# Inverse head norms by one 64-column power on GpSimd and one bounding operation on VectorE, in place of a seed and three Newton steps; row selection one slot later

## The reference

```python
def _head_rmsnorm(x, gamma):
    norm = jnp.linalg.norm(x, axis=-1, keepdims=True)
    normed = x / jnp.maximum(norm, 1e-12)
    scale = (gamma + 1.0) * DIM_HEAD ** 0.5
    return normed * scale[None, :, None, :]
...
x = _rmsnorm(tokens, norm_w)
q = x @ Wq
kv = x @ Wkv
...
q = _head_rmsnorm(q, q_gamma)
k = _head_rmsnorm(k, k_gamma)
sim = jnp.einsum('bhid,bhjd->bhij', q, k)
sim = jnp.tanh(sim / SOFTCLAMP) * SOFTCLAMP * DIM_HEAD ** (-0.5)
out = jnp.einsum('bhij,bhjd->bhid', softmax(sim), v)
```

## Time and profile before

| | |
|---|---|
| median of 3 runs | 1172.26 us (1169.23 to 1201.33) |
| the profiled execution | 1171.93 us, its span 1170.0 us |
| granted TensorE clock, mean | 0.996 |
| PE busy | 1053.4 us (90%) |
| ACT busy | 1033.3 us (88%) |
| DVE busy | 932.8 us (80%) |
| POOL busy | 853.8 us (73%) |

### The profile page before, as it was taken

One profiled execution on the slowest core, in us unless ns is written; L12 is line 12 of the kernel. 1 busy time (PEld: TensorE's weight loads), 2 busy tenths in 40 slices (PEclk: granted clock), 3 DMA queues, 4 the chain that ended last, 5 costly groups with the idle time before them and its releaser, 6 DMA issues.

```text
span 1170.0 us, 33883 instructions
## 1 busy us (share of the span) xinstructions
PE 1053.4 (90%) x12873; PEld 833.1 (71%) x12873; DVE 932.8 (80%) x2185; ACT 1033.3 (88%) x1543; POOL 853.8 (73%) x784
## 2 busy tenths in 40 slices
PE   3779999999999999999999999999999999999987
PEld 2457777777777777777777777777777777777766
DVE  5887878887878878878878878878888878888862
ACT  2689999999999999999999999999999999999886
POOL 6577777778778777778777778777778777778654
PEclk9899999999999999999999999999999999999999
DMA  4244443334433333434334433334333334343341
GB/s 142 42 78 67 77 74 77 68 74 74 77 77 74 70 70 78 74 75 77 72 66 79 76 72 79 66 74 79 74 72 78 71 69 83 70 75 70 71 81 33
DMA packets 310743, 86.45 MB, mean 74 GB/s; under 512 B 282036, under 2 KB 309816, under 8 KB 310584
## 3 DMA queue, kind: packets, MB, share of 16 engines
q1 hardware_dynamic: 310584, 84.30, 37.7%
HBM read 12.13 MB, written 4.19 MB: 14 GB/s over the span
## 4 chain that ended last, share of the span: by engine, by line
ACT 34%; PE 26%; DVE 26%; issue 12%; DMA 0%; POOL 0%; ACTq 0%
ACT clamped L569 12%; PE ps_scores L492 9%; DVE qk L764 7%; ACT probs L576 7%; PE ps_aux L467 5%; DVE halves L728 5%; ACT oT L608 4%; ACT L613 4%; DVE o_sb L741 3%; PE ps_y L542 3%; DVE v_lo L769 3%; DVE norm L679 3%; ACT hid L613 3%; PE ps_y L540 3%; PE ps_aux L426 2%
## 5 line engine op out<-in xcount | busy, mean ns | idle before, releaser
L931 POOL TENSOR_TENSOR probs_lo<-probs 128x1024 f16<-128x1024 f32 x256 | 484.7, 1893 | 270.3 <-ACT probs L576 270.3
L569 ACT ACTIVATE clamped<-ps_scores 128x1024 f32<-128x1024 f32 x256 | 265.9, 1039 | 67.2 <-PE ps_scores L492 66.9
L576 ACT ACTIVATE probs<-clamped 128x1024 f32<-128x1024 f32 x256 | 275.4, 1076 | 1.0 <-PE ps_o L522 0.4
L728 DVE TENSOR_TENSOR halves<-ps_n,halves 128x512 f16<-128x512 f32 x256 | 175.1, 684 | 99.3 <-ACT halves L584 99.2
L520 PEld LDWEIGHTS ps_o<-v_hi,probs 128*128 128x128 bf16 x2048 | 184.7, 98 | 90.0 <-issue 87.5
L520 PE MATMUL ps_o<-v_hi,probs 128*128 128x65 bf16 x2048 | 214.0, 195 | 33.2 <-DVE ps_n L720 23.1
L492 PE MATMUL ps_scores<-heads_T 64*128 64x256 f16 x3072 | 212.8, 271 | 6.9 <-ACT clamped L569 4.7
L521 PE MATMUL ps_o<-v_lo,probs 128*128 128x64 bf16 x2048 | 212.2, 193 | 0.0
L522 PE MATMUL ps_o<-v_hi,probs_lo 128*128 128x65 bf16 x2048 | 211.9, 194 | 0.0
L426 PE MATMUL ps_aux<-w_hi,xhT_hi 128*128 128x512 f32 x384 | 174.4, 454 | 40.0 <-DVE v_lo L769 25.6
L521 PEld LDWEIGHTS ps_o<-v_lo,probs 128*128 128x128 bf16 x2048 | 187.5, 99 | 0.0
(11 more groups left out here) (80 smaller groups left out, 1919.4 us busy)
## 6 DMA issues: line engine op xcount, KB each, us to landing
heads_T<-halves SPq DMA_TRANSPOSE x512, 2.5
x_in<-in_L_attn_tokens_dram SPq DMA_DIRECT2D x32, 128.0 KB, 2.3
x_res<-in_L_attn_tokens_dram SPq DMA_DIRECT2D x32, 128.0 KB, 2.3
out_dram<-y_sb SPq DMA_DIRECT2D x32, 128.0 KB, 2.0
sel_raw<-xn SPq DMA_DIRECT2D x192, 4.0 KB
qk<-in_L_attn_Wkv_dram SPq DMA_DIRECT2D x2, 512.0 KB, 5.2
qk<-in_L_attn_Wq_dram SPq DMA_DIRECT2D x1, 512.0 KB, 4.0
qk<-in_L_ffn_W_dram SPq DMA_DIRECT2D x2, 256.0 KB
```

The costliest lines, as they stand in the source:

```text
L569: nc.scalar.activation(clamped[:].rearrange("p j n -> p (j n)"), ps_scores[:].rearrange("p j n -> p (j n)"), ACT.Tanh).then_inc(clamp_done, 1)
L576: nc.scalar.activation(probs[:, pair % RING].rearrange("p j n -> p (j n)"), clamped[:].rearrange("p j n -> p (j n)"), ACT.Exp, bias=LIFT, ...
L728: v.tensor_tensor(halves16[:, pair % 4, 1].rearrange("p a n -> p (a n)"), ps_n[:], halves16[:, pair % 4, 0].rearrange("p a n -> p (a n)"), ...
L931: g.tensor_tensor(probs_lo[:, buf].rearrange("p j n -> p (j n)"), probs[:, buf].rearrange("p j n -> p (j n)"), probs[:, buf].rearrange("p ...
```

## The change

The two seeds and the nine Newton operations are taken out of VectorE's list. GpSimd gets one instruction in slot 3, `norm_roots`: `norm2` to the power of -0.5, 128 x 64 elements, with the tile `minus_half` grown from 4 to 64 columns as its second input. VectorE gets one instruction in slot 4, `guard`: the minimum of the roots and 1e12, written to `rnorm`. `select` moves from slot 3 to slot 4 of GpSimd's list. The waits of PE on seeds and Newton operations go; the first `normalise` of a batch waits for the guard instead; the first sum of squares of a batch waits until the roots of the batch before are made.

```diff
 VECTOR_STEPS = [
...
-    [("halves",), ("sum", 6, 1), ("sum", 7, 1), ("divide",), ("normalise",), ("seed", 0), ("low", 1, 0), ("seed", 1)],
-    [("halves",), ("divide",), ("newton", 0), ("normalise",), ("newton", 1), ("newton", 2), ("newton", 3), ("newton", 4)],
-    [("halves",), ("divide",), ("newton", 5), ("newton", 6), ("newton", 7), ("newton", 8), ("normalise",), ("norm_stats",),
+    [("halves",), ("sum", 6, 1), ("sum", 7, 1), ("divide",), ("normalise",), ("low", 1, 0)],
+    [("halves",), ("divide",), ("normalise",)],
+    [("halves",), ("divide",), ("guard",), ("normalise",), ("norm_stats",),
      ("q", 0, 2)],
...
     [("bias",), ("lo",)],
+    [("roots",), ("lo",)],
     [("select",), ("lo",)],
-    [("lo",)],
     [("rstd",), ("lo",)],
...
-        minus_half = sb("minus_half", [P, 4])
+        minus_half = sb("minus_half", [P, TT * 2 * HEADS])
...
                 wait(pe, qk_normed, min(PAIRS * n + s - 1 + NORMALISE_LEAD + 1, PAIRS * batches))
-                if s == 3:
-                    wait(pe, seed_made, min(2 * (n + 2), 2 * batches))
-                if s in (4, 5):
-                    wait(pe, newton_step, min(9 * (n + 2) - (4 if s == 4 else 0), 9 * batches))
...
+                if k == 0:
+                    wait(dve, roots_made, b)
                 v.tensor_reduce(norm2[:, 8 * k:8 * k + 8], squares.rearrange("p (h d) -> p h d", d=DH),
                                 AX_X, ALU.add).then_inc(norm2_made, 1)
...
+            def guard(st):
 
                 b, _, _ = st.batch(1)
+                dve.wait_ge(roots_made, b + 1)
+                wait(dve, qk_normed, PAIRS * b)
+                v.tensor_scalar(rnorm, roots[:], NORM_MAX, None, ALU.min).then_inc(rnorm_made, 1)
 
             def normalise(st, ahead, pair):
...
                 if pair == 0:
-                    dve.wait_ge(newton_step, 9 * b + 9)
+                    dve.wait_ge(rnorm_made, b + 1)
...
+            def norm_roots(st):
+
+                b, _, _ = st.batch(1)
+                pool.wait_ge(norm2_made, 8 * b + 8)
+                wait(pool, rnorm_made, b)
+                g.tensor_tensor(roots[:], norm2[:], minus_half[:], ALU.pow).then_inc(roots_made, 1)
```

More of the change, by code:

```diff
@@ L41 @@
 RMS_EPS = 2.0 ** -23
-NORM2_MIN = 1e-24
-RSQRT_SEED = float(0x5F3759DF - (1 << 22) - (1 << 30))
+NORM_MAX = 1e12
 LIFT = 4.1588830833596715
@@ L208, in block_kernel @@
         norm2 = sb("norm2", [P, TT * 2 * HEADS])
-        newton_r = sb("newton_r", [P, TT * 2 * HEADS])
+        roots = sb("roots", [P, TT * 2 * HEADS])
         at = 4 * (DH + 1)
-        rnorm, minus_half_norm2, newton_a = [ps_o[:, at + i * TT * 2 * HEADS:at + (i + 1) * TT * 2 * HEADS] for i in range(3)]
+        rnorm = ps_o[:, at:at + TT * 2 * HEADS]
         halves16 = sb("halves16", [P, 4, 2, TT * 2, P], F16)
@@ L264, in block_kernel @@
         norm2_made = sem("norm2_made")
-        seed_made = sem("seed_made")
-        newton_step = sem("newton_step")
+        roots_made = sem("roots_made")
+        rnorm_made = sem("rnorm_made")
         q_scaled = sem("q_scaled")
@@ L678, in sum_squares @@
                     dve.wait_ge(k_squared, 4 * b + 2 * t + c - 1)
+                if k == 0:
+                    wait(dve, roots_made, b)
                 v.tensor_reduce(norm2[:, 8 * k:8 * k + 8], squares.rearrange("p (h d) -> p h d", d=DH),
                                 AX_X, ALU.add).then_inc(norm2_made, 1)
-            def seed(st, k):
+            def guard(st):
                 b, _, _ = st.batch(1)
[L685 to L709, removed]
+                dve.wait_ge(roots_made, b + 1)
+                wait(dve, qk_normed, PAIRS * b)
+                v.tensor_scalar(rnorm, roots[:], NORM_MAX, None, ALU.min).then_inc(rnorm_made, 1)
             def normalise(st, ahead, pair):
@@ L807, in run @@
                                 normalise(st, *now)
-                        elif what == "seed":
+                        elif what == "guard":
                             if "front" in st.stages:
[L810 to L813, removed]
+                                guard(st)
                         elif what == "norm_stats":
@@ L858, in norm_rstd @@
                 g.tensor_tensor(rstd[:].rearrange("p a b -> p (a b)"), var_eps[:].rearrange("p a b -> p (a b)"),
-                                minus_half[:], ALU.pow).then_inc(rstd_made, 1)
+                                minus_half[:, 0:2 * TT], ALU.pow).then_inc(rstd_made, 1)
             def norm_apply(st, ahead):
@@ L955, in run @@
                                 add_bias(st)
+                        elif what == "roots":
+                            if "front" in st.stages:
+                                norm_roots(st)
                         elif what == "select":
```

## The result

The changed kernel takes 1343.93 us in the median (1342.47 to 1345.01), 1.148 times the kernel before (95% interval 1.146 to 1.150): slower by about 173 us. Its profiled execution took 1343.59 us, with a span of 1341.8 us, 171.7 us more than that of the kernel before. One execution of the kernel before, of 1201.33 us, was a slow one and is left out of the ratio; the others took 1169.23 to 1172.26 us.

A forecast was written before the change was run, and what follows sets the result against it. PE (90% busy) and ACT (88%) were taken to share the bound. 1171.9 us now, plus 254 for 31 full steps of 8.2 us, plus 11 ahead of the first attention gave 1437 us; range 1165 to 1475.

The forecast's parts named there:

- cheap power: GpSimd slot 3: power up to 5 us, guard never waits, time as now, 1160 to 1190 us; chance 0.24.
- the case that I chose: GpSimd slot 3: power's cost goes by the column, 11 to 14.2 us, kernel at 1350 to 1475 us; chance 0.52.
- partly pipelined: GpSimd slot 3: power of 6 to 11 us, a step grows by it less about 5.9 us, 1190 to 1350; chance 0.18.
- What is taken from VectorE counts as nothing: VectorE slots 3 and 4: removing 2.3 us a step of Newton work gains nothing, at most 31.8 us over the run.
- faster: PE at slots 3 and 5: Newton operations held it up, both waits vanish, 1140 us; needs power under 5 us; chance 0.03.
- The length of the power: GpSimd slot 3, 64 columns: 13.7 us, from 0.19 us fixed plus 0.211 us a column; bounds 1.13 and 16.5.
- the upper end: GpSimd power: all of its cost is by the column with nothing fixed, 16.5 us for 64 columns.
- The walk of the step: One full step, GpSimd to PE: lo(3) 7.0 us late, values(4) 8.6 late, less 0.78 regained, so 7.8 us longer.
- The clock: PE behind its idle hole before values(3): low clock for 5.4 us adds 0.4 us a step, at most 1.1.
- The selection: GpSimd slot 4: its 3.7 us now stand between lo(3) and lo(4), so lo(4) ends at 642.8; costs nothing else.
- The new waits: VectorE's guard in slot 4 waits 7.1 us for the power; the first sum of squares' wait is never late.

The follow-up runs named there:

- The cheap product: The changed kernel with the 64-column power replaced by a product of the same two tiles, inverse norms not made: 1167.82 us, 0.9972 of the kernel before.
- the roots that nobody waits for: The kernel before, Newton operations kept, with the unread 64-column power added in GpSimd slot 3 and selection in slot 4: 1341.34 us, ratio 1.1457.

## Why the prediction was right, point by point

The direction and the mechanism were right: the power is long, lo and the values queue behind it, and PE's low clock adds a little. The size was not: the time was forecast at 1437 us and came out at 1344, and the rise at 265 us for about 173. That 1344 lies in the stated range says little, since the range of 1165 to 1475 had to take in the cheap power as well. The own range of the case that I chose, 1350 to 1475, missed it; power and time fall in that of the rival "partly pipelined" (6 to 11 us, 1190 to 1350), to which I had given 0.18.

*What is taken from VectorE counts as nothing.* Right. The cheap product and the two kernels with earlier Newton operations have steps of 34.95 us without those waits, or nearly so. The rival "faster" had the right rows and the wrong reading of them: a wait of 0.69 us in front of a PE that later waits 0.78 us anyway.

*The length of the power.* This is the term that was mis-sized: 13.7 us forecast, 10.56 measured. I had taken the fixed part from the other operations, 0.19 us, and spread all the rest over four columns, 211 ns each. The fixed part is 0.4 us, and a column costs 159. From one row of four columns the two could not be told apart. The cost is nearly in proportion to columns all the same, so the argument for the upper end held and only its size was off. The rival "cheap power" is shut out by the row at 32 columns.

*The walk of the step.* Right once it is given 10.56 us. lo(3) would end at 621.70 + 10.56 + 1.85 = 634.1, values(3) 3.8 us late; lo(4) at 639.65, values(4) 5.46 us late, less 0.78 is 4.7 us. At the full clock, that is with the hole filled, the step is 4.79 us longer. That lo decides and not the guard, which I had left undecided between 7.1 and 7.0 us of lateness, was shown by the roots that nobody waits for.

*The clock.* Forecast 0.4 us a step, with bounds of 0 and 1.1; measured 0.54 in the mean, between 0 and 1.02. The low clock lasted 2.8 to 6.1 us behind the hole, where I had taken 5.4. The sum for the right length is 1171.9 + 31 x (4.7 + 0.4) + 7.9 = 1338 us, and 1343.6 was measured in the profiled execution. So the length of the power explains the miss: it takes 99 us off the forecast, which was 93 us too high.

*The selection.* That it came to stand in front of lo(4) was in the walk, and the three kernels around it show it: 39.73 us a step with it there, 38.01 with it in slot 7, both with the hole filled.

*The new waits.* The guard's took 133 us of VectorE's time, and cost nothing in a full step, as the roots that nobody waits for show. The one of the first sum was never late.

## What to carry to other kernels

Before a calculation is moved to an engine with time to spare, two numbers are to be held against its length: the engine's idle time in a whole step, which caps what any placement can give (8.5 us here against 10.6), and the slack at the place where it is put, which here let 5.4 us pass free and charged 5.3 for 10.6. A special operation such as a power is to be measured at two widths before it is trusted at a third, since a single narrow row doesn't split into a fixed and a running part. And a stall that makes TensorE idle may be paid for twice, here with holes of 5.0 us, once as idle time and once at the low clock behind it, so that undoing one of two causes may show nothing until the other is gone as well.

## What the hardware showed that I had not expected

- The power on GpSimd costs 159 ns a column of 128 partitions and 0.4 us beside, against 1.67 ns a column from the product and the subtraction of the earlier trace rows, some 95 times. At 64 columns the same instruction as a product takes 0.32 us, 33 times less.
- Behind PE's hole, once in each step, the clock's loss went round in a cycle of five steps, 0 to 1.02 us; 18 idle matmuls in the hole took it away, and with the selection out of the way won 66.6 us, 5% of the run.
- VectorE operations of 0.22 us took 1.46 and 3.65 us with their operands in SBUF while GpSimd was at work. The one with two tiles as inputs was held through three GpSimd instructions in a row, the one with a tile and constants only through the one that was running; the whole kernel was 6.4% slower.
